# A mixing matrix made on VectorE in eight multiply-and-add steps instead of on GpSimd

## What is computed

```python
y = x + conv1d(x, weight, 9 taps, 4 groups) + c_weight @ cond + bias      # per sample
att = softmax(MLP(cond))                       # 8 numbers per sample
agg_w = sum_k att[k] * weight[k]               # 128 x 128, a matrix of its own per sample
agg_b = att @ bias_k
out = y + agg_w @ y + agg_b
```

## Time and profile before

| | |
|---|---|
| median of 3 runs | 726.35 us (726.35 to 726.84) |
| the profiled execution | 728.89 us, of it 726.9 us span |
| granted clock of TensorE, mean | 0.998 |
| busy: PE (TensorE) / PEld (weight loads) | 716.2 / 701.7 us |
| busy: DVE (VectorE) / ACT (ScalarE) / POOL (GpSimd) | 462.2 / 601.3 / 546.9 us |
| chain that ended last | PE 81%, POOL 11%, DMA 5% |
| moved by the DMA engines | 177.56 MB, 244 GB/s |

### The profile page before, as it was taken

How to read it: one execution, slowest core, us unless ns; L and a number is a source line. 1 busy time by engine, 2 the same in 40 slices (tenths; PEclk the granted TensorE clock), 3 DMA queues, 4 the chain that set the end, 5 groups by cost and what they waited for, 6 DMA issues and landing times.

```text
span 726.9 us, 29222 instructions
## 1 busy us (share of the span) xinstructions
PE 716.2 (99%) x12417; PEld 701.7 (97%) x12417; DVE 462.2 (64%) x411; ACT 601.3 (83%) x458; POOL 546.9 (75%) x592
## 2 busy tenths in 40 slices
PE   8999999999999999999999999999999999999996
PEld 6799999999999999999999999999999999999996
DVE  4897676576776675575575575575575575575543
ACT  5988888878888888888988888888888988888843
POOL 2799999999999999967767767767767767767750
PEclk9999999999999999999999999999999999999999
DMA  6345858768777877877787778777777767767546
GB/s 208 140 152 200 274 202 281 244 213 298 251 250 261 274 253 248 285 244 246 268 280 260 251 272 294 244 238 275 245 242 275 245 238 275 245 243 271 191 151 243
DMA packets 66551, 177.56 MB, mean 244 GB/s; under 512 B 7437, under 2 KB 50008, under 8 KB 50264
## 3 DMA queue, kind: packets, MB, share of 16 engines
q1 hardware_dynamic: 66002, 176.93, 71.5%
q10 hardware_dynamic: 518, 0.17, 0.1%
HBM read 101.57 MB, written 75.50 MB: 244 GB/s over the span
## 4 chain that ended last, share of the span: by engine, by line
PE 81%; POOL 11%; DMA 5%; SPq 1%; issue 1%; DVE 0%; ACT 0%; DVEq 0%; POOLq 0%; ACTq 0%
PE ps L429 60%; PE ps L460 21%; POOL mix_prod L744 4%; POOL mix_prod L739 4%; DMA mix_dram<-mix_parts 3%; POOL mix_sum_f L747 1%; DMA x_in<-in_x_dram 1%; SPq L290 1%; POOL mix_f L751 1%; DMA mix_rep<-mix_dram 1%; POOL mix_parts L757 1%; POOL mix_parts L754 0%; POOL par L734 0%; POOL par L763 0%; ACT x_hi L512 0%
## 5 line engine op out<-in xcount | busy, mean ns | idle before, releaser
L429 PE MATMUL ps<-x_hi,cw_hi 32*128 32x512 f32 x3072 | 406.0, 387 | 0.8 <-ACT x_hi L512 0.5
L429 PE MATMUL ps<-x_hi,cw_lo 32*128 32x512 f32 x3072 | 405.0, 386 | 0.0
L508 ACT ACTIVATE x_ph<-x_in 128x2560 f32<-128x2560 f32 x63 | 318.7, 5060 | 2.7 <-DMA x_in<-in_x_dram 2.2
L612 DVE TENSOR_TENSOR y_lo<-ps,y_hi 128x512 fp32r<-128x512 f32 x256 | 159.1, 683 | 241.1 <-ACT y_hi L521 241.1
L429 PE MATMUL ps<-x_lo,cw_hi 32*128 32x512 f32 x3072 | 275.6, 385 | 0.0
L429 PEld LDWEIGHTS ps<-x_lo,cw_hi 32*128 32x128 f32 x3072 | 240.0, 183 | 2.3 <-issue 0.8
L429 PEld LDWEIGHTS ps<-x_hi,cw_hi 32*128 32x128 f32 x3072 | 219.5, 184 | 3.8 <-issue 1.6
L429 PEld LDWEIGHTS ps<-x_hi,cw_lo 32*128 32x128 f32 x3072 | 219.1, 184 | 1.6 <-issue 0.2
L460 PE MATMUL ps<-y_hi,mix_rep 32*128 32x512 f32 x2048 | 215.1, 384 | 2.1 <-DMA mix_rep<-mix_dram 2.1
L534 ACT ACTIVATE z_out<-ps,par 128x1024 f32<-128x1024 f32 x124 | 146.5, 1242 | 74.5 <-PE ps L460 74.5
L601 DVE TENSOR_TENSOR x_lo<-x_ph,x_hi 128x2560 fp32r<-128x2560 f32 x63 | 190.0, 3016 | 2.1
(11 more groups left out here) (79 smaller groups left out, 94.9 us busy)
## 6 DMA issues: line engine op xcount, KB each, us to landing
x_in<-in_x_dram SPq DMA_DIRECT2D x64, 1024.0 KB, 7.0
out_dram<-z_out SPq DMA_DIRECT2D x63, 1024.0 KB, 5.0
mix_rep<-mix_dram SPq DMA_DIRECT2D x256, 128.0 KB, 2.7
mix_dram<-mix_parts SPq DMA_DIRECT2D x64, 128.0 KB, 5.7
out_dram<-x_in SPq DMA_DIRECT2D x2, 512.0 KB, 4.0
z_out<-in_L_cond_weight_dram SPq DMA_DIRECT2D x1, 512.0 KB, 4.0
cw_nat<-in_L_cond_weight_dram SPq DMA_DIRECT2D x1, 144.0 KB, 2.2
w_sb<-in_L_cond_W_dram ACTq DMA_DIRECT2D x2, 64.0 KB, 5.0
```

The lines of the kernel that those rows point to most:

```text
L429: mm = pe.matmul(y_at(s)[:, g, :], w[rows, m, :], x_at(xx[buf(s)], rows, m), start=i == 0, stop=i == CONV - 1)
L508: nc.scalar.activation(x_ph[buf(s)][:, :, :, :], by_lane(x_in[buf(s)]), ACT.Copy).then_inc(x_split_ph, 1)
L612: nc.vector.tensor_tensor(y_lo[s[1]][:, g, :], y_at(s)[:, g, :], y_hi[s[1]][:, g, :].bitcast(F32), ALU.subtract).then_inc(y_lo_made, 1)
```

## The change

The mixing matrix moves from GpSimd to VectorE. Two accumulators, `mix_even` and `mix_odd`, take the eight terms in turn: the first is a product, the second a product plus the identity, the other six multiply a matrix by its number from `par` and add it to the accumulator of their parity. The sum of the two is then taken twice, to float32 and rounded to fp32r, and the difference of these is the rest, as before. GpSimd has nothing left to do after the start. On VectorE the matrix of sample 0 is made ahead of x_lo of sample 1; that of every other sample s is made in slot s, after x_lo of s+1 and ahead of y_lo of s. `finish_table`, and the copy of agg_b of sample 0 behind it, move from after y_lo of sample 0 to between x_hi and x_lo of sample 2.

```diff
--- before.py
+++ after.py
@@ -112,8 +112,8 @@
         y_lo = [sb(f"y_lo{k}", [P, G, N], F32R) for k in range(U)]
         z_out = two(sb, "z_out", [P, T])
         par = [sb(f"par{k}", [P, PC]) for k in range(U)]
-        mix_prod = sb("mix_prod", [P, NK, P])
-        mix_sum_f = sb("mix_sum_f", [P, P])
+        mix_even = sb("mix_even", [P, P])
+        mix_odd = sb("mix_odd", [P, P])
         mix_f = sb("mix_f", [P, P])
         mix_parts = two(sb, "mix_parts", [P, 2, P], F32R)
         mix_rep = [sb(f"mix_rep{k}", [P, G, 2, P], F32R) for k in range(3)]
@@ -201,9 +201,8 @@
         y_lo_made = sem("y_lo_made")
         par_made = sem("par_made")
         par_first = sem("par_first")
-        prod_made = sem("prod_made")
+        mix_term = sem("mix_term")
         mix_sum = sem("mix_sum")
-        mix_hi_made = sem("mix_hi_made")
         mix_made = sem("mix_made")
         mix_stored = two(sem, "mix_stored")
         mix_loaded = two(sem, "mix_loaded")
@@ -669,7 +668,6 @@
             nc.vector.tensor_tensor(aggb_prod, ps[:, 6, :].rearrange("p (k s) -> p s k", k=NK),
                                     mixb_t[:, :].unsqueeze(1).broadcast_to([P, NS, NK]),
                                     ALU.add).then_inc(table_made, 1)
-            rest_x((0, 1))
 
             def finish_table():
                 dve.wait_ge(table_made, 2)
@@ -679,16 +677,61 @@
                 dve.wait_ge(table_made, 4)
                 nc.vector.tensor_tensor(table[:, :, NK:NK + 1].rearrange("p s a -> p (s a)"), agg_b[:, :],
                                         ctx_c[:, :], ALU.add).then_inc(table_made, 1)
+                dve.wait_ge(table_made, 5)
+
+            def mix_matrix(s):
+
+                if not exists(s):
+                    return
+
+                at_least(dve, z_read, done(s, 2, lag=-U))
+                a = par[s[1]]
+                if is_sample(s, 0):
+                    dve.wait_ge(table_made, 1)
+                    dve.wait_ge(mixw_copied, 1)
+                    dve.wait_ge(ident_made, 2)
+                    nc.vector.tensor_copy(a[:, 0:NK], table[:, 0, 0:NK]).then_inc(par_first, 1)
+                    dve.wait_ge(par_first, 1)
+                else:
+                    nc.vector.tensor_copy(a[:, :], table[:, number(s), :]).then_inc(par_made, 1)
+                    dve.wait_ge(par_made, done(s))
+
+                for k in range(NK):
+                    part = (mix_even, mix_odd)[k % 2]
+                    if k == 0:
+                        nc.vector.tensor_scalar(part[:, :], mixw_t[:, k, :], a[:, k:k + 1], None,
+                                                ALU.mult).then_inc(mix_term, 1)
+                        continue
+                    if k >= 2:
+                        dve.wait_ge(mix_term, done(s, NK, lag=-1) + k - 1)
+                    nc.vector.scalar_tensor_tensor(part[:, :], mixw_t[:, k, :], a[:, k:k + 1],
+                                                   ident[:, :] if k == 1 else part[:, :],
+                                                   ALU.mult, ALU.add).then_inc(mix_term, 1)
+                dve.wait_ge(mix_term, done(s, NK))
+                nc.vector.tensor_tensor(mix_f[:, :], mix_even[:, :], mix_odd[:, :], ALU.add).then_inc(mix_sum, 1)
+
+                at_least(dve, mix_stored[buf(s)], DMA * uses(s))
+                nc.vector.tensor_tensor(mix_parts[buf(s)][:, 0, :], mix_even[:, :], mix_odd[:, :],
+                                        ALU.add).then_inc(mix_sum, 1)
+                dve.wait_ge(mix_sum, done(s, 2))
+                nc.vector.tensor_tensor(mix_parts[buf(s)][:, 1, :], mix_f[:, :],
+                                        mix_parts[buf(s)][:, 0, :].bitcast(F32),
+                                        ALU.subtract).then_inc(mix_made, 1)
+                dve.wait_ge(mix_made, done(s))
 
             def slot(s):
                 if not is_sample(s, 0):
                     round_x(after(s, 1))
+                    if is_sample(s, 1):
+                        finish_table()
+                        nc.vector.tensor_copy(par[0][:, NK:PC], table[:, 0, NK:PC]).then_inc(par_made, 1)
                     rest_x(after(s, 1))
+                    mix_matrix(s)
                 for g in range(G):
                     rest_y(s, g)
-                if is_sample(s, 0):
-                    finish_table()
-
+
+            mix_matrix((0, 0))
+            rest_x((0, 1))
             pipeline(dve, slot)
 
             dve.wait_ge(par_made, NS)
@@ -721,51 +764,6 @@
                 nc.gpsimd.tensor_copy(cw_hi[:, r:r + K, Q * r:Q * r + Q], wt_hi[:, :, :].bitcast(F32)
                                       ).then_inc(cw_hi_placed, 1)
 
-            def mix_matrix(s):
-
-                if not exists(s):
-                    return
-
-                at_least(pool, z_read, done(s, 2, lag=-U))
-                if is_sample(s, 0):
-                    nc.gpsimd.tensor_copy(par[0][:, 0:NK], table[:, 0, 0:NK]).then_inc(par_first, 1)
-                    pool.wait_ge(par_first, 1)
-                else:
-                    nc.gpsimd.tensor_copy(par[s[1]][:, :], table[:, number(s), :]).then_inc(par_made, 1)
-                    pool.wait_ge(par_made, done(s))
-
-                for k in range(0, NK, NK // 2):
-                    ks = slice(k, k + NK // 2)
-                    nc.gpsimd.tensor_tensor(mix_prod[:, ks, :], mixw_t[:, ks, :],
-                                            par[s[1]][:, ks].unsqueeze(2).broadcast_to([P, NK // 2, P]),
-                                            ALU.mult).then_inc(prod_made, 1)
-                pool.wait_ge(prod_made, done(s, 2))
-                for n, half in enumerate((4, 2)):
-                    nc.gpsimd.tensor_tensor(mix_prod[:, 0:half, :], mix_prod[:, 0:half, :],
-                                            mix_prod[:, half:2 * half, :], ALU.add).then_inc(mix_sum, 1)
-                    pool.wait_ge(mix_sum, done(s, 3, lag=-1) + n + 1)
-                nc.gpsimd.tensor_tensor(mix_sum_f[:, :], mix_prod[:, 0, :], mix_prod[:, 1, :],
-                                        ALU.add).then_inc(mix_sum, 1)
-                pool.wait_ge(mix_sum, done(s, 3))
-
-                nc.gpsimd.tensor_tensor(mix_f[:, :], mix_sum_f[:, :], ident[:, :], ALU.add)
-
-                at_least(pool, mix_stored[buf(s)], DMA * uses(s))
-                nc.gpsimd.tensor_tensor(mix_parts[buf(s)][:, 0, :], mix_sum_f[:, :], ident[:, :],
-                                        ALU.add).then_inc(mix_hi_made, 1)
-                pool.wait_ge(mix_hi_made, done(s))
-                nc.gpsimd.tensor_tensor(mix_parts[buf(s)][:, 1, :], mix_f[:, :],
-                                        mix_parts[buf(s)][:, 0, :].bitcast(F32),
-                                        ALU.subtract).then_inc(mix_made, 1)
-                pool.wait_ge(mix_made, done(s))
-                if is_sample(s, 0):
-                    pool.wait_ge(table_made, 5)
-                    nc.gpsimd.tensor_copy(par[0][:, NK:PC], table[:, 0, NK:PC]).then_inc(par_made, 1)
-
-            pool.wait_ge(table_made, 1)
-            pool.wait_ge(mixw_copied, 1)
-            pipeline(pool, mix_matrix)
-
 
 # ---- launch: one core; inputs and outputs as the reference has them ----
 _INS = ["x", "cond_128", "fside_S_0", "L0_cond_weight", "L0_cond_c_weight", "L1_cond_W0", "L1_cond_b0",
```

## The result

The changed kernel takes 734.88 us in the median of six runs (734.01 to 735.67), the kernel before beside it 726.66 us (726.35 to 730.34). The ratio is 1.0082, 95% interval 1.0056 to 1.0108: slower by 0.8%. The forecast was 733.7 us, the range 730.0 to 737.2. The profiled execution took 735.24 us with a span of 733.5, 6.6 us over that of before; the medians are 8.2 us apart, because single executions of the kernel before scatter widely: between 725.0 and 733.9 us over all 86 that stand beside the runs of this study.

The account below looks back on a forecast made before the run. TensorE, busy 99%, was taken to bound the kernel, with VectorE last to finish at the start. Start +8.0, clock +2.4 and late stalls -3.1 gave +7.3 us on 726.35, so 733.7 us; range 730.0 to 737.2.

Parts of the forecast that it names:

- The start, +8.0 us: Ahead of sample 2's first y_lo: three matrices on VectorE, less relief from silent GpSimd, start sample 3 8.0 us later.
- Rival 2: In making matrices on VectorE: no operations overlap, 4.0 us a matrix, 2.2 us more, 735.9 us; chance 0.08.
- The clock, +2.4 us: Sample 3, behind TensorE's stall: matmuls run at 1.2 GHz for 5 to 5.5 us, net +2.4 us.
- Rival 1: At the stall before sample 3: the clock holds, +4.9 us, 731.2 us; chance 0.15.
- The late stalls, -3.1 us: At samples 7, 11 and 12 to 13: TensorE's waits for the mixing matrix from DRAM go, -3.1 us.
- rival 4: Whole kernel not slower: only the late stalls go and the start is cheap; 726.0 us at 1.5 us a matrix; chance 0.08.
- rival 5: The late stalls stay because the way of store and loads makes them, not GpSimd: +3.1 us, 736.8 us; chance 0.06.
- The cover in the steady state, 1.5 us: From sample 4 on: VectorE can take 1.5 us more per sample before TensorE is delayed.
- Rival 3: Steady state: VectorE becomes the bound, from 4.75 us a matrix; 770 us at 5.25 us a matrix; chance 0.03.
- The tail: End of the kernel: as before, since the last matrix is needed long after it is made.

Follow-up runs that it names:

- three matrices on GpSimd: Against the kernel before: GpSimd makes the matrices of samples 0 to 2, VectorE those of samples 3 to 63; 730.09 us, ratio 1.0032.
- spread handover: Against the kernel before: GpSimd makes the first four or three matrices, VectorE the rest, moved ahead of y_lo gradually over several samples; 728.34 and 728.56 us.
- The run with 1.31 us more: The change with five more multiply-and-add steps per matrix on VectorE from sample 8 on, results unused; 752.58 us, ratio 1.0328.
- the spread handover with four: Against the kernel before: GpSimd makes matrices 0 to 3, VectorE the rest, behind y_lo in sample 4, wholly ahead from sample 7; 728.34 us, ratio 0.9990.
- the matrix's store first: The spread handover with four, with SyncE storing the matrix ahead of the two large transfers from sample 4 on; 727.13 us, ratio 0.9983 against the kernel before.

## Why the prediction was right, and where it was not

**The start, +8.0 us**: +8.14 measured, 7.77 of it from the start of sample 1 on. The rest, 0.37 us, was there before any matrix could matter and differs from one execution to the next, so that the agreement to 0.14 us is partly luck. A matrix was put at 3.25 us and takes 3.21; x_hi is at 1.48 us with GpSimd silent, as forecast; TensorE begins sample 2 0.8 us late for x_hi (0.9 forecast); the stall is 6.5 us by the waits, 7.0 by the window (6.8 forecast). The estimate of 3.4 us a matrix by the formula of the Trainium skill, page "VectorE: DVE Perf Modes", section "The TRN2 errata — SBUF-src ops pay a fixed extra latency per instruction", would have put sample 3 some 0.5 us later. For one operation the trace agrees with it (292 ns for a sum of 128 columns, 291 by the formula), but consecutive terms overlap by 0.08 us. Rival 2, nothing overlaps, falls by the same rows.

**The clock, +2.4 us**: +2.1 measured, 13.25 us against 11.14. The clock fell in the stall and 4.87 us passed at half of it, where 5 to 5.5 were expected. Rival 1 falls, and the kernel that kept TensorE busy shows that the term is the clock's. The rule of the Trainium skill, page "TensorE: Matmul & The Clock Gate", section "HAM oscillation — how this bites in real kernels", that stalls of TensorE are paid a second time in cold matmuls, held for this stall; in the profiled run with three matrices on GpSimd it did not, the clock stayed at 1.00 behind a stall of 2.4 us.

**The late stalls, -3.1 us**: -3.14 measured, **but the step behind it was half wrong**. The prediction said that they go because the matrix is ready 12 us sooner, and that no transfer in the queue is held. The two kernels with a spread handover still waited for matrices that were ready 8 to 10 us after their sample's start, and the kernel whose matrices GpSimd makes from sample 3 on did not wait. What counts is how far behind SyncE's queue is, and by these runs it is ahead in the change because TensorE stood at the start. The two terms are not independent: with a start that cost nothing, as in the two spread handovers, most of the stalls would have stayed. That the term came out to 0.04 us is therefore partly luck: its sizes were read off the trace of before, whose slots lose 3.1 us in all, and its cause was only half the one given. That also weakens rival 4, which joined a cheap start to the end of the stalls; rival 5 had named the queue, but not what releases it.

**The cover in the steady state, 1.5 us: wrong.** The step took the matrix's 0.7 us of room and added 0.8 us between the last y_lo and TensorE's next sample. The run with 1.31 us more should have cost nothing by it and cost 0.36 us in each sample. The cover is 0.95 us, about VectorE's idle time: what the step missed is that VectorE works in a loop, where a late y_lo also makes the x_hi and x_lo behind it late, so that the 0.8 us cannot be used up anew in each sample. This is the likeliest reading and not shown; with five more terms VectorE still waits 0.2 us a sample for y_hi, so ScalarE is part of the loop. Rival 3 decides from 4.2 us a matrix (3.21 + 0.95), not 4.75. It changed nothing at 3.21 us, but the margin was two thirds of what was said.

**The tail**, forecast as unchanged, is 0.5 us shorter in these two profiles, 23.6 us from the start of sample 63 against 24.1. This is no effect of the change: in the kernels that end like the change it takes from 23.7 to 24.7 us.

**The median**: the 7.3 us of the sum stand against 6.6 between the spans and 8.2 between the medians. The sum itself is 8.14 + 2.12 - 3.14 - 0.5 = 6.6 us, in which the 0.37 us ahead of sample 1 and the 0.5 us of the tail are scatter.

## What to carry to other kernels

Before moving work to an engine with idle time, look at the start: where that engine is already the last to finish, each microsecond comes out at the end, and a stall of TensorE may be paid again in the clock. When a wait goes away together with a new stall elsewhere, ask if the stall gave a queue the time to catch up; a loop of store, landing and load that takes about as long as a sample gives back a delay only over many samples. Do not add two slacks of one engine that works in a loop: here its idle time per turn was all there was. And before reading a difference of half a microsecond between two profiles, look where in the program it arises: here as much stood ahead of the change and in the tail.

## What the runs showed of the hardware

- Beside GpSimd's work VectorE's short operations lose far more of their speed than long ones: a copy of 9 columns took 1.26 and 1.00 us in place of 0.17, a multiply-and-add of 128 columns 0.55 to 0.61 in place of 0.35, and x_lo of 2560 columns 3.5 in place of 2.8. In these rows the difference is 0.2 to 1.1 us for an operation, and no larger for the long one than for the copy.
- TensorE's clock fell to 1.2 GHz (granted share 0.50) behind stalls of 6.5, 3.9 and 1.7 us; in the profiled run with three matrices on GpSimd it stayed at 2.4 GHz (1.00) behind one of 2.4 us, and in the spread handover with four behind one of 1.6 us. The length of the stall alone did not decide it in these five.
- A store of 128 x 256 numbers landed 7.3 to 9.5 us after its issue when it stood right behind two transfers of 1 MB, in four turns of the spread handover with four (4.9 to 7.6 us in the change, for samples 3 to 12). Ahead of these transfers, with the matrix's store first, it landed after 1.7 to 4.6 us (samples 4 to 12).
